# Routing shortened, the last batch's turns reordered, an expert chunk loaded earlier, scatters in order 4, 3, 2, 0, 1

## The reference: two mixers, then a mixture of experts

```
r1  = bi_wkv(x, fside, fside, w, u, cond)      # forward and backward decaying sums, ratio, sigmoid
x   = x + attn(r1)                             # 3 projections, a gated linear recurrence, W_out
r2  = bi_wkv(x, fside, fside, w2, u2, cond)
# mixture of experts over the S = 2048 rows of r2: 8 experts, top 2, capacity C = 640 rows each
probs = softmax(r2 @ Wg);  gate, expert = top_k(probs, 2)
pos   = position of a row within its expert;  kept = pos < 640
h     = relu(rows_of_expert @ w1[e])           # 512 -> 2048
y     = h @ w2[e]                              # 2048 -> 512
out   = x + sum over the row's kept experts of gate * y
```

## Time and profile before

| | us |
|---|---|
| median of three runs (lowest, highest) | 1123.8 (1121.9, 1128.33) |
| the profiled execution's own time | 1130.62 |
| its span in the profile | 1128.8 |
| PE busy (share) | 1040.3 (92%) |
| DVE busy | 644.6 (57%) |
| ACT busy | 519.7 (46%) |
| POOL busy | 279.3 (25%) |
| mean granted TensorE clock | 0.969 of full speed |

### The profile page before, as it was taken

The page is one execution under the profiler, slowest core; times in us unless marked ns, Lnnn a source line. Parts: engine busy times, 40 slices in busy tenths (PEclk is TensorE's granted clock), DMA queues, the critical chain, the costliest instruction groups (busy, mean ns, idle before and its releaser), DMA issues.

```text
span 1128.8 us, 17219 instructions
## 1 busy us (share of the span) xinstructions
PE 1040.3 (92%) x5034; PEld 816.5 (72%) x5035; DVE 644.6 (57%) x939; ACT 519.7 (46%) x836; POOL 279.3 (25%) x232
## 2 busy tenths in 40 slices
PE   3599997999996899999999999999999999999993
PEld 2334543454455799989998999898887888899892
DVE  5899999999982333343334333555564344334551
ACT  6776774677632233343334333445553334334441
POOL 4665748634654000030002000300203002000202
PEclk9999898999988899999999999999999999999997
DMA  6991432224414422262226222634536225222521
GB/s 212 315 308 30 112 72 89 53 69 113 136 39 169 146 74 74 74 167 75 74 74 168 74 74 74 172 144 166 165 114 213 74 74 158 89 92 90 137 74 22
DMA packets 67104, 131.34 MB, mean 116 GB/s; under 512 B 4966, under 2 KB 6026, under 8 KB 67080
## 3 DMA queue, kind: packets, MB, share of 16 engines
q1 hardware_dynamic: 53856, 105.25, 26.8%
q0 software_dynamic: 13008, 25.52, 11.5%
q10 hardware_dynamic: 216, 0.28, 0.1%
HBM read 90.66 MB, written 35.22 MB: 112 GB/s over the span
## 4 chain that ended last, share of the span: by engine, by line
PE 64%; issue 1%; POOL 1%; DVEq 0%; DVE 0%; ACT 0%; POOLq 0%
PE ps_y L1595 11%; PE ps_y L1596 11%; PE ps_y L1597 11%; PE ps_h L1575 10%; PE ps_h L1576 10%; PE ps_h L1577 10%; PE ps_t L1545 1%; POOL out_dram L1524 1%; DVEq L1650 0%; DVE y L1797 0%; DVE hl L1774 0%; ACT y L1719 0%; DVE gate L1759 0%; DVEq L1773 0%; DVEq L1763 0%
## 5 line engine op out<-in xcount | busy, mean ns | idle before, releaser
L1575 PE MATMUL ps_h<-xh,w1h 128*128 128x320 f32 (+4 forms) x768 | 245.0, 319 | 7.7 <-issue 7.1
L1576 PE MATMUL ps_h<-xl,w1h 128*128 128x320 f32 (+4 forms) x768 | 241.3, 314 | 0.0
L1577 PE MATMUL ps_h<-xh,w1l 128*128 128x320 f32 (+4 forms) x768 | 241.2, 314 | 0.0
L1524 POOL DMA_INDIRECT out_dram<-y,token x40 | 63.8, 1594 | 642.4 <-DVE y L1797 402.2
L1774 DVE SCALAR_TENSOR_TENSOR hl<-ps_h,hh 128x320 fp32r<-128x320 f32 (+1 forms) x192 | 107.2, 558 | 191.9 <-ACT hh L1702 187.1
L1595 PE MATMUL ps_y<-w2h,hh 128*128 128x512 f32 x528 | 207.1, 392 | 0.8 <-issue 0.5
L1596 PE MATMUL ps_y<-w2h,hl 128*128 128x512 f32 x528 | 206.3, 391 | 0.0
L1597 PE MATMUL ps_y<-w2l,hh 128*128 128x512 f32 x528 | 206.1, 390 | 0.0
L1702 ACT ACTIVATE hh<-ps_h 128x320 fp32r<-128x320 f32 (+1 forms) x192 | 94.2, 491 | 234.6 <-PE ps_h L1577 231.2
L1737 DVE TENSOR_TENSOR w2l<-raw,w2h 128x512 fp32r<-128x512 f32 x127 | 87.8, 692 | 196.6 <-ACT w2h L1679 195.6
L1679 ACT ACTIVATE w2h<-raw 128x512 fp32r x127 | 80.1, 631 | 210.2 <-PE ps_y L1597 210.2
(11 more groups left out here) (206 smaller groups left out, 1163.8 us busy)
## 6 DMA issues: line engine op xcount, KB each, us to landing
raw<-in_L_ffn_w_dram SPq DMA_DIRECT2D x64, 1024.0 KB
slots<-r_rows SPq DMA_DIRECT2D x8, 1302.5 KB, 22.6
rows<-slots SPq DMA_DIRECT2D x7, 1302.5 KB
rows<-in_x_dram SPq DMA_DIRECT2D x4, 1024.0 KB, 5.2
sums_even<-eukv POOLq DMA_DIRECT2D x8, 512.0 KB, 5.1
sums_odd<-eukv POOLq DMA_DIRECT2D x8, 512.0 KB, 5.3
out_dram<-rows SPq DMA_DIRECT2D x4, 1024.0 KB
f_rows<-in_fside_BxSxS_dram SPq DMA_DIRECT2D x3, 1024.0 KB, 6.6
```

The costliest lines, as they stand in the source:

```text
L1575: nc.tensor.matmul(o, w1h[:, j, dt, :], xh[:, dt, lo:hi], start=(dt == 0), stop=False)
L1576: nc.tensor.matmul(o, w1h[:, j, dt, :], xl[:, dt, lo:hi], start=False, stop=False)
L1577: last = nc.tensor.matmul(o, w1l[:, j, dt, :], xh[:, dt, lo:hi], start=False, stop=(dt == CT - 1))
```

## The change

- `select`: no copy of the logits, they are read from PSUM. Only the two best indices are cast (`top_f` is now 128 x 2 x 4) and later multiplied by the capacity.
- `place`: the base of the expert is added at the end, from `top_f`. The two products of `slot_f` and one-hot are issued without a wait between them, the two reductions become one.
- Last batch on PE: `logits_tile(3)` stands ahead of `r2_tile(0)`; `r2_tile(1)`, `places(3)`, `r2_tile(2)` and `r2_tile(3)` ahead of the four `x2_row`, which now come after the count matmul. `r2_tile` signals each row by itself. ACT has the same order and makes the high parts of the first weights before `probabilities(3)`; DVE makes the first low part between `select(3)` and `place(3)`.
- SP loads chunk 1 of expert 0 before `store(3)`, when the mixers' buffers are free, instead of behind the first expert's rows.
- Scatters, `down` and the evictions go in order 4, 3, 2, 0, 1. A skipped tile is signalled by PE at the expert's first hidden tile instead of the last; in the variant for up to 512 rows ACT signals tile 4 with its last hidden tile.
- 38 instead of 30 unread matmuls.

```diff
@@ sync_program @@
         load_chunk(sp, load_sems[0], place0[0][:, 0], place0[1][:, 0], w1, w2, 0, 0)
         store(2)
+        sp.wait_ge(s_bwd, 2 * len(UNITS))
+        sp.wait_ge(s_eukv, len(UNITS))
+        sp.wait_ge(load_sems[0], 32)
+        load_chunk(sp, load_sems[0], place0[0][:, 1], place0[1][:, 1], w1, w2, 0, 1)
         store(3)
@@ r2_tile @@
-            last.then_inc(s_to_r2, 1)
+                if ct == CT - 1:
+                    last.then_inc(s_to_r2, 1)
@@ tensor_program, end @@
         logits_tile(2)
+        logits_tile(3)
         r2_tile(0)
-        logits_tile(3)
+        r2_tile(1)
+        places(3)
+        r2_tile(2)
+        r2_tile(3)
+        pe.wait_ge(s_dest, B)
+        nc.tensor.matmul(ps_count, ones[:], carry[:], start=True, stop=True).then_inc(s_count, 1)
         x2_row(3, 0)
...
         x2_row(3, 3)
-        places(3)
-        r2_tile(1)
-        r2_tile(2)
-        r2_tile(3)
-        pe.wait_ge(s_dest, B)
-        nc.tensor.matmul(ps_count, ones[:], carry[:], start=True, stop=True).then_inc(s_count, 1)
+        pe.wait_ge(s_ev_r2, TT * B)
@@ r2_row on ACT @@
-            act.wait_ge(s_to_r2, TT * b + (i + 1 if b < B - 1 else TT))
+            act.wait_ge(s_to_r2, TT * b + i + 1)
@@ scalar_program, end: the first pieces, probabilities(3), r2_row(3, 0..3), x2_row(3, 0..3) @@
@@ select @@
-            st.do(v.tensor_copy(logit[:], logit_of(b)))
+            logit = logit_of(b)
...
-            st.do(v.tensor_copy(top_f[:], top_i[:]))
+            st.do(v.tensor_copy(top_f[:], top_i[:, :, 0:TOPK].rearrange("p i k -> p k i")))
...
+            st.mark(v.tensor_scalar(top_f[:], top_f[:], float(CAP), None, ALU.mult))
@@ place @@
-            st.do(v.tensor_scalar(slot_t[:], ps_pos, float(CAP), float(NO_TOKEN), ALU.is_ge, ALU.mult))
-            st.do(v.tensor_tensor(slot_f[:], ps_pos, slot_t[:], ALU.add))
-            st.do(v.tensor_tensor(slot_f[:], slot_f[:], slot_base[:], ALU.add))
+            st.do(v.tensor_scalar(slot_f[:], ps_pos, float(CAP), float(NO_TOKEN), ALU.is_ge, ALU.mult))
+            st.do(v.tensor_tensor(slot_f[:], ps_pos, slot_f[:], ALU.add))
             for k in range(TOPK):
-                st.do(v.tensor_tensor(slot_t[:], slot_f[:], oh[:, k], ALU.mult))
-                st.do(v.tensor_reduce(dest_f[:, k], slot_t[:], AX.X, ALU.add))
-            st.do(v.tensor_tensor(carry[:], carry[:], sel_sum[:], ALU.add))
-            v.tensor_copy(dest[:, b % 2], dest_f[:]).then_inc(s_dest, 1)
+                st.mark(v.tensor_tensor(slot_t[:, k], slot_f[:], oh[:, k], ALU.mult))
+            st.mark(v.tensor_tensor(carry[:], carry[:], sel_sum[:], ALU.add))
+            st.wait()
+            st.do(v.tensor_reduce(dest_f[:], slot_t[:], AX.X, ALU.add))
+            v.tensor_tensor(dest[:, b % 2], dest_f[:], top_f[:], ALU.add).then_inc(s_dest, 1)
@@ vector_program, end @@
         select(3, routing[3])
+        first_low(0)
         place(3, routing[3])
...
+        first_low(1)
+        first_low(2)
@@ experts @@
-    EVEN_ORDER, ODD_ORDER = (2, 4, 0), (3, 1)
+    EVEN_ORDER, ODD_ORDER = (4, 2, 0), (3, 1)
...
-        sp.wait_ge(s_w, 32)
-        weights(sp, 0, 1, 1)
...
-            for i in (*range(2, ST), 0, 1):
+            for i in (*range(ST - 1, 1, -1), 0, 1):
@@ down @@
-            for i in range(2, ST):
+            for i in range(ST - 1, 1, -1):
                 with pe.If(count > i * P):
...
-                if last:
+                if first:
                     with pe.Else():
                         pe.sem_inc(s_out[i], 1)
...
-        for n in range(30):
+        for n in range(38):
@@ ACT, last hidden tile of an expert @@
                             with act.If(c > NC - 2):
+                                if not wide:
+                                    act.wait_ge(s_token, e + 1)
+                                    act.sem_inc(s_ya, 1)
...
-                for i in EVEN_ORDER if wide else (2, 0):
+                for i in EVEN_ORDER if wide else EVEN_ORDER[1:]:
```

More of the change, by code:

```diff
@@ L205, in conditioning_and_routing @@
     rows_of = lambda b: last_rows if b == B - 1 else r2_rows
-    logit = sb("logit", [P, TT, NE])
     top = sb("top", [P, TT, NE])
     top_i = sb("top_i", [P, TT, NE], U32)
-    top_f = sb("top_f", [P, TT, NE])
+    top_f = sb("top_f", [P, TOPK, TT])
     oh = sb("oh", [P, 2, TT, NE])
@@ L218, in conditioning_and_routing @@
     slot_f = sb("slot_f", [P, TT, NE])
-    slot_t = sb("slot_t", [P, TT, NE])
+    slot_t = sb("slot_t", [P, TOPK, TT, NE])
     dest_f = sb("dest_f", [P, 2, TT])
@@ L267, in conditioning_and_routing @@
     N_VEC = N_V + 1
-    ROUTE_STEPS = 17 + 2 * TT
+    ROUTE_STEPS = 15 + 2 * TT
     REC_STEPS = 1 + CT
@@ L465, in tensor_program @@
     def tensor_program(pe):
-        pe.wait_ge(s_pool_setup, 9)
+        pe.wait_ge(s_pool_setup, 8)
         def vec_turn():
@@ L1087, in scalar_program @@
         exponentials()
[L1088 to L1091, removed]
+        act.wait_ge(load_sems[0], 32)
+        act.wait_ge(s_bwd, 2 * len(UNITS))
+        for raw, high, _, which in first_pieces(place0):
+            a.activation(high, raw, ACT.Copy).then_inc(load_sems[2 + 2 * which], 1)
         probabilities(3)
@@ L1096, in scalar_program @@
         r2_row(3, 3)
[L1098 to L1101, removed]
+        x2_row(3, 0)
+        x2_row(3, 1)
+        x2_row(3, 2)
+        x2_row(3, 3)
     def vector_program(dve):
@@ L1248, in select @@
             st.wait()
-            v.tensor_tensor(pe_[:], logit[:], bc(top[:, :, 0:1]), ALU.subtract).then_inc(s_shift, 1)
+            v.tensor_tensor(pe_[:], logit, bc(top[:, :, 0:1]), ALU.subtract).then_inc(s_shift, 1)
             for i in range(TT):
@@ L1392, in vector_program, with first_low @@
         select(3, routing[3])
+        def first_low(n):
+            raw, high, low, which = first_pieces(place0)[n]
+            dve.wait_ge(load_sems[2 + 2 * which], n + 1 if which == 0 else 1)
+            v.tensor_tensor(low, raw, high.bitcast(F32), ALU.subtract).then_inc(load_sems[3 + 2 * which], 1)
+        first_low(0)
         place(3, routing[3])
@@ L1397, in vector_program @@
         dve.wait_ge(s_count, 2)
-        for n, (raw, high, low, which) in enumerate(first_pieces(place0)):
-            dve.wait_ge(load_sems[2 + 2 * which], n + 1 if which == 0 else 1)
-            v.tensor_tensor(low, raw, high.bitcast(F32), ALU.subtract).then_inc(load_sems[3 + 2 * which], 1)
+        first_low(1)
+        first_low(2)
+        dve.wait_ge(s_ev_r2, TT * B)
     return {"sync": sync_program, "gpsimd": gpsimd_program, "tensor": tensor_program,
@@ L1436, in experts @@
     s_y0, s_h0 = sem("y_cleared"), sem("hidden_cleared")
-    s_out = {i: sem(f"output_tile_{i}_done") for i in (2, 3, 4, 0)}
+    s_out = {i: sem(f"output_tile_{i}_done") for i in (4, 3, 2, 0)}
     WIDE = 512
@@ L1715, in body @@
                 act.wait_ge(s_token, e + 1)
-                for i in EVEN_ORDER if wide else (2, 0):
+                for i in EVEN_ORDER if wide else EVEN_ORDER[1:]:
                     act.wait_ge(s_out[i], e + 1)
-                    a.activation(y[:, i], ps_y[:, i, :], ACT.Copy, scale=gate[:, i:i + 1]).then_inc(
-                        s_ya, 2 if i == 2 and not wide else 1)
+                    a.activation(y[:, i], ps_y[:, i, :], ACT.Copy, scale=gate[:, i:i + 1]).then_inc(s_ya, 1)
             by_width(act, e, body)
```

7 lines of the change are left out of this document (2 added, 5 removed).

## The result

The changed kernel takes 1119.47 us in the median, the kernel before 1126.84 measured beside it (eight runs each). One run of the changed kernel, 5872 us, was disturbed: it is among the eight of that median (1119.29 without it) and counts nowhere else. The ratio is 0.9939, 95% interval 0.9920 to 0.9957: faster by 6.9 us, 4.8 to 9.0 (the two medians stand 7.4 apart). Forecast were 1113.8 us and 10.0 us less. The sign was right; the time lies 5.7 us above the forecast and half a microsecond outside its range.

A forecast was written before the change was run, and what follows sets the result against it. PE bounds the experts (113.89 of 115.00 us busy), so only first program, bridge and tail can gain. Bridge 4.7 + first program 3.3 + tail 2.7 - skips 0.7 = 10.0; 1123.8 - 10.0 = 1113.8 us, range 1109.5 to 1119.

The forecast's parts named there:

- the last one: Closing sum: takes the 10.0 us from the runs' median of 1123.8, not the profiled 1130.62, giving 1113.8 us.
- Bridge to `dest`: Last batch's routing after the logits: `dest` at 346.0 instead of 350.19, 4.2 us earlier (3.0 to 4.6).
- Bridge from `dest`: From `dest` through scatters and row fetch to the first expert matmul: 0.5 us shorter, by turns at full clock.
- Skips on PE: Skips before the first tile in experts' first and last `down`: 0.7 us charged (0 to 2).
- skips in the way: Rival: skips delay PE in every `down`, 23.5 us more if none is hidden, 1137 us; chance 0.04.
- First program: Shorter `select` and `place` in batches 0 to 2: 3.3 us saved, from 0 to 3.9.
- Tail: Scatters behind the last matmul: last one starts 2.3 to 2.9 us earlier, taken as 2.7.
- Store(3) sets the fetch: Rival: the bridge's output store holds up the row fetch, gain 7, 1116.8 us; chance 0.14, shared with the clock.
- No shorter bridge: Rival: ACT's pieces or PE's turns hold `dest`, only tail and first program count, 1118.5 us; chance 0.08.
- The first program gives nothing: Rival: the shorter routing in the first program saves nothing, 10.0 - 3.3, 1117.1 us; chance 0.15.
- reads no second tensor: Shortened `place(1)`: all but its last step ends before POOL's work or has one input; 2.3 us saved.

The follow-up runs named there:

- e2: Kernel before with only the new order of PE, ACT and DVE at the end of the first program, long routing steps kept: 1125.05 us, ratio 0.9984.
- e3: Kernel before with only the new order of scatters, downs and evictions and the earlier signals for skipped tiles: 1125.42 us, ratio 0.9991.
- e5: Kernel before cut to experts 0 and 1, the six others left out: 616.09 us, five runs.
- e7: Changed kernel cut to experts 0 and 1, with the long selection and placing in batches 0, 1 and 2: 616.28 us, five runs.
- e9: Changed kernel at full length with the long selection and placing in batches 0, 1 and 2: 1119.88 us, 12 runs.
- e15: Kernel before once more, unaltered, for a second full profile: 1129.19 us.
- e1: Kernel before with only select and place shortened, in all four batches: 1125.03 us, ratio 0.9983.
- e4: Changed kernel again, unaltered, for a second profile: 1119.49 us, ratio 0.9935 against the kernel before.
- e6: Changed kernel cut to experts 0 and 1, the six others left out: 610.21 us, five runs.
- e8: Changed kernel at full length with 52 unread matmuls in place of 38: 1121.07 us.
- e10: Changed kernel once more, unaltered, as anchor of its group: 1118.34 us, 6 runs.
- e11: Changed kernel with the weights of chunk (0, 1) loaded behind the row loads, as before: 1118.80 us, 11 runs.
- e12: Changed kernel where POOL reads the last expert's count and leaves out scatters of tiles 3 and 4 that hold no token: 1118.59 us, 6 runs.
- e16: Changed kernel once more, unaltered, for profile and median in the last group: 1119.43 us.
- e13: Changed kernel with the long selection and placing in batch 0 alone: 1120.14 us.
- e14: Changed kernel with the long selection and placing in batch 1 alone: 1118.04 us, six runs.

## Why the prediction was off

**The step that failed is the last one**, "the terms are pauses and DVE steps that do not depend on that difference, so 1123.8 - 10.0". It has two faults, and together they put the time 0.5 us outside the range.

*The base.* 1123.8 was the median of three runs, 6.4 us apart. Over all its runs the kernel before has a mean of 1127.5 us in 101 runs (standard deviation 3.0), the changed one 1119.0 in 27 (1.5). Of the miss of 5.7 us, 3.0 is the base alone (1126.84 against 1123.8 in the first comparison), 2.6 the sum (10.0 against 7.4). Over all runs the change is worth 8.4 us.

*The terms do depend on it.* The spread between runs is made in the first program and, less, in the bridge, by just the waits and stretched steps that the terms were read from. From the fetch to the last matmul, the fifteen profiles of full kernels lie between 745.3 and 747.1 us, whatever the edit. The end of the logits does not hold still:

| routing of batches 0 to 2 | logits end, us | mean | clamp behind place(1), us |
|---|---|---|---|
| long: before, e2, e3, e5, e7, e9, e15 | 341.45, 335.42, 338.33, 340.81, 341.40, 340.26, 340.88 | 339.8 | 3.64, 1.07 (e2), 3.63, 3.64, 3.64, 3.64, 3.63 |
| short: after, e1, e4, e6, e8, e10, e11, e12, e16 | 334.44, 336.33, 336.77, 334.77, 336.73, 336.09, 334.04, 336.03, 334.46 | 335.5 | 1.13 in all |
| long in batch 0 (e13); in batch 1 (e14) | 337.23; 334.30 | | 1.13; 1.07 |

The profile that I read lay 3.1 us above the mean of its kernel, near the late end, and the first profile after lay 3.1 below that of its own. I took a late run's rows for every run's.

Term by term, with the profiles of the unmixed kernels (before: two; changed: four) and the means of the runs:

- *Bridge to `dest`: 4.2 forecast, 2.5 found.* This is the term that missed most. Logits to `dest` is 8.74, 7.11, 7.44 and 7.70 us where the bridge is the old one (before, e15, e3, e5), mean 7.75, and 4.61, 5.37, 5.41, 5.57 in the changed kernel, mean 5.24. The forecast of 4.5 for the new chain held in its best run; the others begin the selection 0.5 us behind the logits instead of 0.03, and the positions step waits another 0.4 for PE:
```profile
334.95 0.39 DVE L1251 MAX8 top<-ps_decay 128x8 f32<-128x8 f32 x4 [2.05 <-PE ps_decay L580]
338.75 0.19 DVE L1281 TENSOR_SCALAR slot_f<-ps_small 128x32 f32<-128x32 f32 x1 [0.41 <-PE ps_small L615]
```
  (these two rows are e16's). The old chain's 8.74 was its longest case: in e15 ACT's copies came closer together, and DVE waited 2.13 us for the exponentials, not 3.72:
```profile
345.52 0.19 DVE L1270 TENSOR_REDUCE prob_sum<-prob 128x4 f32<-128x32 f32 x1 [2.13 <-ACT prob L871]
```
- *Bridge from `dest`: 0.5 forecast.* `dest` to fetch gained 0.4 (13.2 in the mean of the same four to 12.7; e15 alone has 12.65). Fetch to last matmul 746.0 before, 745.7 after. The turns gained nothing that lasted: a shorter stretch at the half clock is met by a longer pause at the slow branch of `up` (in the first profile 2.8 us at the half clock and then 2.17 of pause, in e4 5.9 and 0.79), and in e8 the branch stands ahead of the first matmul.
- *Skips on PE: 0.7 charged, nothing found*, since fetch to last matmul holds both. The rival "skips in the way" fell with it, at full size: 23 us would show in any profile.
- *First program: 3.3 forecast.* 4.3 between the means of the profiles, 6.1 between the medians of e7 and e6, 1.5 between those of e9 and e10. What the other terms leave of the 8.4 is 1.9, counting that the changed kernel spends 2.16 us outside its span and the old one 1.81 (8.4 + 0.35 - 2.9 - 0.3 - 3.65). So the runs at full length put it near 2, not 3.3, and its size changes with the run. The split was wrong too. I gave batch 1 2.3 us and batch 0 the rest, while batch 1 alone is worth nothing in its profile (e14), batch 0 some 1.7 in its own (e13), and the 2.5 us of the clamp come where POOL starts early enough beside a long `place(1)`, so that the clamp meets its products; in the profiles that is so only with the long routing in both, and not in all of those (e2). The clamp was in the trace of before, three rows behind place(1), and I did not ask why two instructions took 3.64 us.
- *Tail: 2.7 forecast, 3.65 found* (19.98 to 16.33). I gave tile 4's scatter 0.9 us behind ACT's last hidden copy, and it starts 0.5 behind it (1093.56 + 0.60 to 1094.64). Tile 3's eviction (1094.86) waits for no signal of PE any more, and its scatter follows 1.87 behind tile 4's. That is 3.4 of the 3.65; the rest stands behind the last scatter. The last scatter starts 4.5 us behind PE's last matmul, where I had 5.0 to 5.6. The term is in every profile whose last expert has the new order, e3's among them.
- *The rivals.* "Store(3) sets the fetch" fell: issued at 343.15, 8.7 us before the fetch. "No shorter bridge" fell. "The first program gives nothing" (1117.1) was the nearest: in some runs it gives nothing or little, in others 4 us and more, and not because the next wait swallows it. e9's two clusters of runs, 1118.8 and 1123.9 in their medians, suggest both: the first stands beside the changed kernel's 1118.3, and e2's profile, with the clamp at 1.07 us and the logits at 335.42, shows what such an early run of the long routing can look like.

The Trainium skill (SBUF — State Buffer, section "SBUF: two separate sides") holds that of a GpSimd instruction and a DVE one in a 2-port mode or with two SBUF inputs, whichever begins first keeps their shared ports for its whole instruction. The two `slot_t` products above agree with it: 0.08 us ahead of POOL one took 0.20 us, 0.15 behind another took 1.16. The clamp does not. Here the clamp's second instruction has 0.43 us of start on POOL's product and ends behind it and the next one (291.79 + 3.23 = 295.02, POOL until 294.72). The trace agrees that one waits out the other and speaks against the order of claims here, as far as its starts can be trusted. The prediction had only the part of the rule on two inputs. The casts that end the long placing (1.20 us in e14, 0.17 as an addition in the changed kernel's free stretch) have one input, so my "reads no second tensor" was no shelter either.

What stays open: which rows make the early half of before's runs, since only seven profiles with the long routing in batches 0 to 2 exist and six of them show the clamp stalled; and whether the kernel before differs by chip (medians of 1126.8 in the first comparison, 1126.8, 1126.8, 1126.1 and 1129.4 in the four groups; the changed kernel 1119.5 in the first comparison and 1119.5, 1118.3 and 1119.4 in three groups). What the eight more unread matmuls are worth was not measured by itself. No kernel tried here is faster than the changed one by more than its runs can tell.

## What to carry to other kernels

A saving read from one profile is a saving for that run: when the profiled execution stands several microseconds off the median, find where the runs differ before adding up, and look first at whether the terms themselves lie there. Where several engines release each other in fine steps, fewer small steps can be worth more for where the next long step then falls than for their own time (here 0.2 to 0.4 us decided over 3.5), and the same cut in two batches need not be worth twice the cut in one. Steps in a stretch that holds still from profile to profile (the tail here) can be sized from one.

## What the runs showed of the hardware

- Two DVE clamps of 128x512 between SBUF tiles took 1.07 to 1.13 us or, with POOL's two products beside them, 3.63 to 3.64, and no time between, in eighteen profiles.
- A DVE product of 128x32 took 0.19 to 0.20 us where it started 0.07 to 0.08 us ahead of a POOL product (e2, e14), and 1.02 to 1.18 where it started 0.13 to 0.29 behind it (before, e3, e5, e7, e9, e15).
- The kernel before spreads over 12.6 us in 101 runs, the changed one over 5.1 in 27, with the same matmuls but for the eight more that nobody reads.
- One compare-and-branch in PE's queue, in the first pass through the loop, took 2.57 to 3.60 us in each of the eighteen profiles, where the median on its line is 0.20 (e8 has another of 1.25). With fourteen more matmuls ahead of the turns (e8) it came before the first expert matmul, which then started 4.66 us behind the last split instead of 1.76 to 1.80.
- A run's own time less its span goes with the kernel: 1.80 and 1.82 us in two profiles of the one before, 2.13 to 2.18 in four of the changed one. Small edits of it have either (1.72 in e12, 2.21 in e11).
